# Attention and ternary feed-forward on one core: x rows of the last chunks loaded earlier, own buffers for chunk 5, another order of the end

## What is computed

```python
x = layernorm(x + attention(x, w_qkv, w_out, b_out, w_th))
x = layernorm(x + ffn(x, w_up, w_down))

def attention(x, ...):            # 16 heads of 64, blocks of 16 tokens
    q, k, v = split(x @ w_qkv)    # token 0 of a sequence is "bos": its output is its v
    # each block of 16 queries sees the bos token and 5 blocks (2 before, itself, 2 after),
    # later keys masked; softmax over them
    attn = einsum('gh,bhnij->bgnij', w_th, softmax(sim))   # mix over heads
    return (attn @ v) @ w_out + b_out

def ternary_linear(x, w):         # w_t in {-1, 0, 1}
    w_t = sign(w) * (abs(w) > 0.5 * mean(abs(w)))
    return (x / (rms(x) + 1e-8)) @ w_t.T
ffn = ternary_linear(gelu(ternary_linear(x, w_up)), w_down)    # 128 -> 512 -> 128
```

## Time and profile before

| | |
|---|---|
| median of 3 runs | 278.1 us (276.99 to 279.89) |
| profiled execution, time | 278.77 us |
| its span, first to last instruction | 276.2 us |
| mean granted TensorE clock | 0.952 of full speed |
| busy: TensorE, weight loads, VectorE, ScalarE, GpSimd | 228.5, 204.3, 187.1, 162.2, 96.5 us |

### The profile page before, as it was taken

How to read it: one execution, slowest core, us unless ns; L and a number is a source line. 1 busy time by engine, 2 the same in 40 slices (tenths; PEclk the granted TensorE clock), 3 DMA queues, 4 the chain that set the end, 5 groups by cost and what they waited for, 6 DMA issues and landing times.

```text
span 276.2 us, 9860 instructions
## 1 busy us (share of the span) xinstructions
PE 228.5 (83%) x4258; PEld 204.3 (74%) x4258; DVE 187.1 (68%) x486; ACT 162.2 (59%) x306; POOL 96.5 (35%) x114
## 2 busy tenths in 40 slices
PE   1888988999999999989998999899987898428460
PEld 1787876778899898879887988898876787427450
DVE  0465588878676875688567856785778875176780
ACT  1475455666656569745975697569745268007541
POOL 6032432421332251535262625262536210055150
PEclk9999999999999999999999999999999799959855
DMA  7743640010020001001001100110010000100001
GB/s 230 214 116 97 225 101 2 13 50 0 5 58 3 21 13 52 0 25 52 9 1 42 51 12 0 44 41 21 0 43 2 0 4 2 39 19 2 0 29 49
DMA packets 18622, 11.67 MB, mean 42 GB/s; under 512 B 2004, under 2 KB 17940, under 8 KB 18452
## 3 DMA queue, kind: packets, MB, share of 16 engines
q1 hardware_dynamic: 17872, 9.94, 12.3%
q10 hardware_dynamic: 708, 1.12, 1.4%
HBM read 8.91 MB, written 2.10 MB: 40 GB/s over the span
## 4 chain that ended last, share of the span: by engine, by line
PE 44%; DVE 20%; ACT 18%; issue 12%; DMA 2%; POOL 1%; POOLq 0%; DVEq 0%; ACTq 0%
PE bank L1039 7%; PE bank L1041 6%; PE bank L1040 6%; PE bank L1158 5%; PE bank L1184 5%; DVE CTl L829 5%; ACT Yb L552 4%; ACT CTh L552 3%; DVE AT L834 2%; PE bank L1142 2%; DVE E L843 2%; DMA xq<-in_L_attn_x 2%; ACT L636 2%; PE bank L1254 2%; DVE mx L841 2%
## 5 line engine op out<-in xcount | busy, mean ns | idle before, releaser
L484 POOL TENSOR_TENSOR E<-E,rc 128x400 f32<-128x400 f32 x32 | 27.9, 872 | 83.7 <-DVE rc L851 83.6
L829 DVE TENSOR_TENSOR CTl<-bank,CTh 128x512 fp32r<-128x512 f32 x64 | 41.1, 685 | 22.2 <-ACT CTh L552 21.7
L552 ACT ACTIVATE Yb<-bank 128x512 f32<-128x512 f32 x64 | 38.3, 599 | 29.1 <-PE bank L1041 28.5
L1039 PE MATMUL bank<-xTh,Gh 128*128 128x256 f32 x128 | 39.8, 311 | 7.7 <-ACT Yb L552 6.4
L1039 PE MATMUL bank<-CTh,Mh 128*128 128x256 f32 x128 | 37.3, 292 | 4.0 <-DVE CTl L829 2.8
L680 ACT ACTIVATE E<-E 128x400 f32<-128x400 f32 x32 | 17.3, 539 | 39.2 <-DVE E L843 39.0
L552 ACT ACTIVATE CTh<-bank 128x512 fp32r<-128x512 f32 x64 | 34.7, 599 | 5.2 <-PE bank L1184 4.9
L1040 PE MATMUL bank<-CTl,Mh 128*128 128x256 f32 x128 | 36.3, 284 | 0.9 <-issue 0.9
L1041 PE MATMUL bank<-CTh,Ml 128*128 128x256 f32 x128 | 36.3, 284 | 0.0
L1040 PE MATMUL bank<-xTl,Gh 128*128 128x256 f32 x128 | 35.8, 280 | 0.0
L1041 PE MATMUL bank<-xTh,Gl 128*128 128x256 f32 x128 | 35.7, 279 | 0.0
(11 more groups left out here) (137 smaller groups left out, 477.8 us busy)
## 6 DMA issues: line engine op xcount, KB each, us to landing
raw<-in_L_attn_x SPq DMA_DIRECT2D x36, 64.0 KB
w_sb<-in_L_attn_w_qkv ACTq DMA_DIRECT2D x2, 512.0 KB, 5.7
pt_rows<-PT SPq DMA_DIRECT2D x1, 1024.0 KB, 5.6
R<-pt_rows SPq DMA_DIRECT2D x1, 1024.0 KB, 4.9
xr<-in_L_attn_x SPq DMA_DIRECT2D x6, 128.0 KB
out<-y SPq DMA_DIRECT2D x6, 128.0 KB, 2.3
raw<-in_L_attn_x SPq DMA_DIRECT2D x12, 56.0 KB
xq<-in_L_attn_x SPq DMA_DIRECT2D x2, 256.0 KB, 5.6
```

Source lines behind the costliest of these rows:

```text
L484: tt(e, e, rc[s % 2][:, :].unsqueeze(2).broadcast_to([P, TILES, WIN]), ALU.mult).then_inc(s_norm, 1)
L552: copy = lambda o, i, **k: nc.scalar.activation(o, i, ACT.Copy, **k)
L829: v.tensor_tensor(ct_view(CTl[s // 4 % 2], s % 4, q), c_view(s, q), ct_view(f32(CTh[s // 4 % 2][:, :, :]), s % 4, q), ALU.subtract).then_i ...
L1039: mm(o, wh, rh, start=start, stop=False, **k)
```

## The change

- `xr` becomes a pair: the old buffer for chunks 0 to 6, and for chunk 7 a view of `raw`, free once the last window has been split (`s_xwl` at 8). Chunk 7 gets a semaphore of its own. SyncE issues both loads directly after the loop over the windows, ahead of `store(3)`.
- Chunk 5 gets its own `gT`, `gTh`, `gTl` (`gset`: 2 for chunk 5, 1 for chunk 6, 0 for the rest). `up(5)` goes between the first and the second quarter of the projection of chunk 7, and `gelu(5)` and `hidden_high(5)` move forward with it.
- `hidden_low(4)` moves from GpSimd to VectorE and `squares(5)` from GpSimd to ScalarE. The squares of chunk 7 go into `gT5`.
- In the loop, ScalarE's `squares` (k = 4) move behind `y_out(s, 1)` and `down_out`, and VectorE's `result_shift` (k = 7) behind `total` and `second_sum`.
- The rest of the end is reordered on TensorE, ScalarE, VectorE and GpSimd.

```diff
-        xr = sb("xr", [P, CT, P])
+        xr = [sb("xr", [P, CT, P]), raw[:, 0:CT, :]]
...
         def squared(n):
-            return gT[0] if n < 4 else gsq
+            return gT[0] if n < 4 else gsq if n < 7 else gT[2]
+
+        def gset(n):
+            return {5: 2, 6: 1}.get(n, 0)
...
             def residual_rows(n):
-                need(sp, f_res, n)
+                if n < CHUNKS - 1:
+                    need(sp, f_res, n)
+                else:
+                    sp.wait_ge(s_xwl, CHUNKS)
...
-            store(CHUNKS - 5)
             residual_rows(CHUNKS - 2)
             residual_rows(CHUNKS - 1)
-            for n in range(CHUNKS - 4, CHUNKS - 1):
+            for n in range(CHUNKS - 5, CHUNKS - 1):
                 store(n)
```

Behind the loop, GpSimd:

```diff
             variance_roots(6)
-            hidden_low(4, 0)
-            hidden_low(4, 1)
             variance_roots(7)
-            squares(5)
             hidden_root(4)
             last_root(4)
             hidden_root(5)
+            last_root(5)
             hidden_root(6)
-            last_root(5)
             hidden_root(7)
```

ScalarE, `gelu`:

```diff
-                elif n != 6:
-                    act.wait_ge(f_gl, 10 if n == 5 else 12)
-                    act.wait_ge(f_sum, 10 if n == 5 else 12)
+                elif n == 7:
+                    act.wait_ge(f_gl, 10)
```

ScalarE, in the loop:

```diff
-                for n, k in ffn(s):
-                    if k == 4 and n < 4:
-                        squares(n, 0)
-                        squares(n, 1)
                 y_out(s, 1)
...
                     if k == 4 and n < 4:
                         down_out(n)
+                        squares(n, 0)
+                        squares(n, 1)
```

ScalarE, behind the loop:

```diff
             squares(4, 1)
+            gelu(5, 0)
+            gelu(5, 1)
+            hidden_high(5, 0)
+            hidden_high(5, 1)
             result(3)
             stage(7)
-            gelu(5, 0)
             x1_hi(6)
-            gelu(5, 1)
             down_out(4)
-            hidden_high(5, 0)
-            hidden_high(5, 1)
             gelu(6, 0)
             gelu(6, 1)
+            down_out(5)
             x1_hi(7)
             hidden_high(6, 0)
             hidden_high(6, 1)
+            squares(5, 0)
+            squares(5, 1)
             gelu(7, 0)
             gelu(7, 1)
             hidden_high(7, 0)
             hidden_high(7, 1)
-            down_out(5)
             squares(6, 0)
```

VectorE, in the loop:

```diff
-                    if k == 7:
-                        result_shift(n)
                     if k == 2:
                         x1_lo(n)
...
                     if k == 5:
                         second_sum(n)
+                    if k == 7:
+                        result_shift(n)
```

VectorE, behind the loop:

```diff
             residual(6)
             layernorm(5)
+            hidden_low(4, 0)
+            hidden_low(4, 1)
             input_scale(6)
             up_input(6)
+            hidden_low(5, 0)
+            hidden_low(5, 1)
             residual(7)
             x1_lo(6)
             layernorm(6)
             input_scale(7)
             up_input(7)
-            hidden_low(5, 0)
-            hidden_low(5, 1)
             hidden_sum(4)
+            second_sum(4)
             x1_lo(7)
-            second_sum(4)
             hidden_low(6, 0)
             hidden_low(6, 1)
+            second_norm(4)
+            hidden_sum(5)
             layernorm(7)
+            second_sum(5)
             hidden_low(7, 0)
             hidden_low(7, 1)
-            second_norm(4)
-            hidden_sum(5)
-            second_sum(5)
-            hidden_sum(6)
             second_norm(5)
             result_shift(4)
+            hidden_sum(6)
             second_sum(6)
```

TensorE, behind the loop:

```diff
             o_part(7, 0)
+            up(5, 0)
+            up(5, 1)
             o_part(7, 1)
             o_part(7, 2)
             o_part(7, 3)
             x1_T(6)
             attn_back(7)
-            up(5, 0)
-            up(5, 1)
             down(4)
+            down(5)
             up(6, 0)
             up(6, 1)
             down_back(4)
             square_sum(4)
             x1_T(7)
+            down_back(5)
             up(7, 0)
             up(7, 1)
-            down(5)
             square_sum(5)
-            down_back(5)
             down(6)
```

More of the change, by code:

```diff
@@ L140, in attention_ffn @@
         with ExitStack() as last:
+            high5 = last.enter_context(nc.sbuf_tensor("gTh5", [P, FT, CHUNK], F32R))
+            low5 = last.enter_context(nc.sbuf_tensor("gTl5", [P, FT, CHUNK], F32R))
             gT.append(last.enter_context(nc.sbuf_tensor("gT6", [P, FT, CHUNK], F32)))
@@ L143, in attention_ffn @@
             gTl.append(last.enter_context(nc.sbuf_tensor("gTl6", [P, FT, CHUNK], F32R)))
+            gT.append(last.enter_context(nc.sbuf_tensor("gT5", [P, FT, CHUNK], F32)))
+            gTh.append(high5)
+            gTl.append(low5)
             gsq = last.enter_context(nc.sbuf_tensor("gsq", [P, FT, CHUNK], F32))
@@ L187, in attention_ffn @@
         s_O = sem("s_O")
-        s_xr = sem("s_xr")
+        s_xr = [sem("s_xr"), sem("s_xr_last")]
         f_stage, f_aT, f_res, f_st, f_var, f_vin, f_roots, f_rms, f_inv, f_rn, f_x1n, f_x1 = map(sem, (
@@ L496, in hidden_low @@
                 o = slice(2 * t, 2 * t + 2)
-                tt(gTl[n == 6][:, o, :], gT[n == 6][:, o, :], f32(gTh[n == 6][:, o, :]), ALU.subtract).then_inc(f_gl, 1)
+                tt(gTl[gset(n)][:, o, :], gT[gset(n)][:, o, :], f32(gTh[gset(n)][:, o, :]), ALU.subtract).then_inc(f_gl, 1)
             def hidden_root(n):
@@ L508, in last_root @@
                 tt(rstd2[n % 2][:, :], var2[:, :], exps[:, 0, :], ALU.pow).then_inc(f_rstd2, 1)
[L510 to L516, removed]
             for s in range(STEPS):
@@ L641, in hidden_high @@
                 act.wait_ge(f_gelu, 2 * n + t + 1)
-                need(act, f_dn, {6: 0, 7: 6}.get(n, n))
+                need(act, f_dn, {5: 0, 6: 0, 7: 5}.get(n, n))
                 o = slice(2 * t, 2 * t + 2)
-                copy(gTh[n == 6][:, o, :], gT[n == 6][:, o, :]).then_inc(f_gh, 1)
+                copy(gTh[gset(n)][:, o, :], gT[gset(n)][:, o, :]).then_inc(f_gh, 1)
             def squares(n, t):
@@ L651, in squares @@
                     act.wait_ge(f_gl, 2 * n + t + 1)
-                else:
-                    act.wait_ge(f_ss, n)
-                nc.scalar.activation(squared(n)[:, o, :], gT[n == 6][:, o, :], ACT.Square).then_inc(f_sum, 1)
+                elif n < 7:
+                    act.wait_ge(f_ss, n)
+                else:
+                    act.wait_ge(f_gl, 12)
+                nc.scalar.activation(squared(n)[:, o, :], gT[gset(n)][:, o, :], ACT.Square).then_inc(f_sum, 1)
             def down_out(n):
@@ L855, in residual @@
                 dve.wait_ge(f_aT, n + 1)
[L856 removed]
+                dve.wait_ge(s_xr[n == 7], rows_done(n) if n < 7 else 16 * row_parts(n))
                 if n < CHUNKS - 2:
@@ L859, in residual @@
                 v.tensor_tensor(res[own(n)][:, :, :], at_bank(n)[:, 0:CHUNK].rearrange("p (t c) -> p t c", t=CT),
-                                xr[:, :, :], ALU.add).then_inc(f_res, 1)
+                                xr[n == 7][:, :, :], ALU.add).then_inc(f_res, 1)
                 dve.wait_ge(f_res, n + 1)
@@ L900, in hidden_high @@
                 o = slice(2 * t, 2 * t + 2)
-                v.tensor_copy(gTh[n == 6][:, o, :], gT[n == 6][:, o, :]).then_inc(f_gh, 1)
+                v.tensor_copy(gTh[gset(n)][:, o, :], gT[gset(n)][:, o, :]).then_inc(f_gh, 1)
             def hidden_low(n, t):
@@ L906, in hidden_low @@
                 o = slice(2 * t, 2 * t + 2)
-                v.tensor_tensor(gTl[n == 6][:, o, :], gT[n == 6][:, o, :], f32(gTh[n == 6][:, o, :]), ALU.subtract).then_inc(f_gl, 1)
+                v.tensor_tensor(gTl[gset(n)][:, o, :], gT[gset(n)][:, o, :], f32(gTh[gset(n)][:, o, :]), ALU.subtract).then_inc(f_gl, 1)
             def hidden_sum(n):
@@ L1235, in down @@
                     pe.wait_ge(f_gl, 2 * n + k // 2 + 1)
-                    mm(o, wdT[:, k, :], gTh[n == 6][:, k, :], start=(k == 0), stop=False)
-                    ins = mm(o, wdT[:, k, :], gTl[n == 6][:, k, :], start=False, stop=(k == FT - 1))
+                    mm(o, wdT[:, k, :], gTh[gset(n)][:, k, :], start=(k == 0), stop=False)
+                    ins = mm(o, wdT[:, k, :], gTl[gset(n)][:, k, :], start=False, stop=(k == FT - 1))
                 ins.then_inc(f_dn, 1)
```

11 lines of the change are left out of this document (5 added, 6 removed).

## The result

The changed kernel takes 267.8 us (median of 4 runs, 267.31 to 270.05) against 278.6 (276.99 to 279.89): ratio 0.963, 95% interval 0.956 to 0.971, 10.8 us less. Its profiled execution took 267.91 us, with a span of 266.1 against 276.2.

The account below looks back on a forecast made before the run. TensorE was taken to bound the loop, and the tail to wait for x rows whose DMA stood behind a store. Tail 10.6, clock -0.2 and loop 2.1 sum to 12.5 us off 278.1: 265.6 us, range 262.4 to 270.5.

Parts of the forecast that it names:

- (a): Tail: x rows for chunks 6 and 7 in by about 224 us, against needs at 232.19 and 239.9 us.
- (b): Tail: residual(6) starts 8.2 us earlier, at 232.2; x1n(6) done at 236.8, hidden_low(5) till 238.1.
- (c): Tail: projection of chunk 7, lengthened 0.95 us by up(5), sets the pace; residual(7) at 239.9, 7.8 us earlier.
- (d): End of kernel: residual(7) to the end takes 20.0 us instead of 22.8, gaining 2.8 over (c), 10.6 in all.
- (e): Tail: TensorE's lower clock around up(7) and the square sums costs 0.2 us, bounds 0 to 3.
- (f): Loop: Yb waits in steps 16, 20, 24 and result_shift's wait in step 30 go: 2.1 us gained, bounds 0 to 3.6.
- The rule on the shared SBUF interfaces: Tail: VectorE and GpSimd contend when a VectorE instruction has two SBUF inputs; hidden_low(4) and roots(6) delayed at most 1.03 us.
- rival 2: Loop gives nothing, the time TensorE saves being lost again at the next wait: 267.7 us; chance 0.12.
- the slower case: Loop steps 16, 20, 24 and 28: squares end so late that TensorE stands at square_sum: 287.7 us; chance 0.03.
- The third: More than forecast: loop gains 1.5 us more, up(7) fast and tail hand-overs cheaper, 0.6 together: 263.5 us; chance 0.09.
- One sign of being wrong: Tail: up(7) later than 14 us after attn_back(6) because second_sum(4) stands ahead of x1_lo(7).
- rival 4: Same as the slower case: stops reach 2.5 us, where the clock falls, costing 5.0 us four times: 287.7 us; chance 0.03.

Follow-up runs that it names:

- rows_only: The kernel before with only the x row loads changed (both ahead of store(3), chunk 7's into the view of raw): 269.3 us, ratio 0.969.
- own_low5: The changed kernel without the wait for down(4) ahead of hidden_low(5) on VectorE: 265.0 us, ratio 0.953.
- shift_old: The changed kernel with only result_shift moved back to the head of its step in the loop: 269.3 us, ratio 0.967.
- squares_old: The changed kernel with only the loop's squares moved back ahead of y_out(s, 1): 270.5 us, ratio 0.970.
- loop_old: The changed kernel with both moves inside the loop (squares and result_shift) undone: 269.8 us, ratio 0.969.
- rows_loop: The kernel before with the x row loads and both loop moves changed, nothing else: 267.3 us, ratio 0.960.
- squares_later: own_low5 with the loop's squares one step later on ScalarE and square_sum behind the projection part on TensorE: 262.9 us, ratio 0.942.
- low7_first: own_low5 with x1_lo(7) ahead of second_sum(4) on VectorE: 265.0 us, ratio 0.952.
- rows_late: The changed kernel with store(3) again ahead of the two row loads on SyncE: 279.3 us, ratio 1.004.
- clock_fill: own_low5 with 12 matmuls of unused result added on TensorE ahead of up(7): 264.4 us, ratio 0.950.

## Why the forecast came out as it did

The forecast was 265.6 us, in a range of 262.4 to 270.5, and 267.8 was measured: the direction and the main term were right, the time 2.2 us short, one fifth of the gain.

- (a) Right: the rows were there, residual(6) started 0.03 us after attn_back(6). By rows_only the row loads alone are worth 8.9 us.
- (b) Half right. The rms pair took 0.34 and x1n(6) came 4.5 us after residual(6), as counted (236.8 - 232.2 = 4.6). The sentence "hidden_low(5) till 238.1" failed. I took its inputs to be gTh(5) alone and did not look through its waits, one of which is for down(4), behind the projection.
- (c) The projection with up(5) inside took its 0.95 more and is what x1_T(6) waited for. But "residual(7) at 239.9", 7.7 after residual(6), was 10.0, since hidden_low(5) stands ahead of it in VectorE's queue. own_low5 measured 7.8. This is the step that failed: a wait that the change should have dropped and did not, and everything queued behind it.
- (d) From residual(7) to the end 20.0 + 0.2 was forecast and 20.1 measured. Here the agreement is not luck: second_sum(5) ended 11.1 us after residual(7) (10.9 forecast), second_norm(7) 18.7 (18.4).
- (e) The clock did fall in up(7), and VectorE waited 0.67 us for the square sum of chunk 5. In shift_old the clock fell 1 us later, this wait is absent, and the end is 0.3 us shorter: about the 0.2 that was forecast. An earlier fall costs more, 1.8 us in squares_old, inside the bound of 3.
- (f) 2.1 forecast, 2.9 in the trace, 2.0 by loop_old and by rows_loop against rows_only. The parts were not all as I had them. 0.9 in step 30 came (2.77 to 1.85), and the clock held behind it, which is worth another 0.5: from the fourth Yb wait of this kind to the end of attn_back(6) it took 42.35 us before, 40.95 after, and 41.89 in rows_only, with the old wait and the clock held. How much of this 0.5 the shorter wait brought is open. From the Yb wait near 107 us to its like in the next chunk, 27.70 us became 26.43: the 0.36 of step 16 and 0.9 of idle time behind the square sum, which I had not counted. Part of that is the trace: rows_only, with the loop of before, took 26.99. The two chunks after that gained 0.15 and 0.05 only, where I had 0.36 and 0.54: TensorE waited for x1n and x1Tl instead, since ScalarE and VectorE set the pace there. That is the mechanism of rival 2, true for these two chunks. squares_later, which takes the squares out of that stretch, shortened each by 0.9 (27.21 in own_low5 to 26.26, 27.39 to 26.46), though it removed the idle time there as well.
- The rule on the shared SBUF interfaces (Trainium skill, GPSIMD Engine Reference, Specifications): roots(6) ran from 231.79 for 1.03 us, hidden_low(4) on VectorE from 232.13 for 1.29, overlapping for 0.7 us, and both took the times that they had before. So this trace does not agree for that pair: it does not show contention between a power on 128x4 elements and a subtract with two SBUF inputs. It does show it between GpSimd's subtract of 128x512 and the tiny rms pair (2.43 before, 2.49 in rows_only).
- Of the rivals none came true as written, and that 267.8 falls on the 267.7 of rival 2 is an accident: the loop's gain came, and the tail's fell short. That the loop gives nothing is spoken against by two pairs of kernels, 2.0 us each (neither quite clear of its intervals by itself), with the Yb waits and the longer wait for CTl back in the rows wherever a move is undone; and the slower case by the absence of any wait for squares at a square sum. The third lay nearer in the loop than the forecast did, but the wait for down(4) outweighed it.
- One sign of being wrong did appear: up(7) started 16.5 us after attn_back(6) (246.66 - 230.18), with 14 named as the limit. The cause named with it was not the one: 2.2 us were the wait for down(4), and without it (own_low5) it was 14.3. Taking second_sum(4) from ahead of x1_lo(7) (low7_first) brought it to 13.3 and gained nothing.

## What to carry to other kernels

When a tile gets a buffer of its own, list every wait that guarded the shared one, on every engine. Here two of three were changed (in ScalarE's gelu and hidden_high), the third stayed in VectorE's hidden_low and cost 2.8 us, no less than the new order was worth. A forecast of a reordering has to walk through the waits of each moved instruction, not only its inputs. And a load that needs nothing late does not belong in a queue behind a store that does: its place on SyncE, with a second buffer for the last chunk, was 8.9 of 10.8 us. What such a queue costs can also grow by a reordering elsewhere: in rows_late the store came 2.4 us later because result(3) had moved back on ScalarE.

## What else the runs showed

Behind the square sums in the loop TensorE had idle time that no semaphore in the trace explains (released by "issue"): 1.27, 0.86, 0.72 and 0.87 us in steps 16, 20, 24 and 28 of the kernel before, 3.7 in all. With both loop moves undone in the changed kernel it was 1.31, 1.14, 0.86 and 0.55; in the changed kernel 0.31, 0.25 and 0.33, with none of note in step 16. It varies with the trace too: 2.4 to 3.9 us in all in the four kernels with the squares in their old place (2.4 in rows_only, whose loop is that of before), 0.9 to 2.4 in the eight that have them behind down_out, none at all in the two with the square sum behind the projection part. So it goes in the main with the place of the squares and the square sum, and the traces do not say which of the two. Its cause was not tested and stays open.

The pause ahead of CTl in step 30 is the same experiment fourteen times, since each trace has it and the work around it is nearly the same. In four traces it is 2.77 to 2.84 us. The granted clock fell to 0.50 behind it in three (before, loop_old, shift_old) and stayed at 1.00 in rows_only:

```profile
215.69 0.39 PE L1041 MATMUL bank<-CTh,Mh 128*128 128x256 f32 x1 [2.78 <-DVE CTl L831]
```

In ten traces it is 1.84 to 1.86 us. The clock stayed at 1.00 in seven, the changed kernel among them. It fell in low7_first from the first matmul on, and in squares_old and clock_fill 1 to 2 us later:

```profile
214.51 0.45 PE L1042 MATMUL bank<-CTh,Mh 128*128 128x256 f32 x1 [1.86 <-DVE CTl L829]
```

In the tail the same pause of 1.73 us ahead of up(7) left the first matmul at 0.38 in own_low5 and found it at 0.58 in squares_later. So neither the length of the last pause nor the program decides by itself whether the clock falls. That it is low behind a wait of 2.5 us and more, as rival 4 and the expectation of shift_old assume, did not hold in rows_only, and in shift_old it fell late. A forecast can price the low clock (0.4 to 0.5 us here for the 12 matmuls of step 30) and give it a chance, but not place it.
